# Cross-attention with low-rank updates: value and denominator products of a half batch as one run, and key parts placed by transfers on chip

## The reference

```python
def lin(x, W, A, B):          # low-rank update, R = 16
    return x @ W + 2.0 * (x @ A @ B)
q = lin(x, Wq, Aq, Bq)        # 32 heads
k = lin(ctx, Wk, Ak, Bk)      # 8 heads, each serves 4 query heads
v = lin(ctx, Wv, Av, Bv)
p = softmax(q @ k.T / sqrt(32))
out = x + lin(concat_heads(p @ v), Wo, Ao, Bo)
```

## Time and profile before

| | us |
|---|---|
| median of 3 runs | 1055.89 |
| runs | 1052.37 to 1056.95 |
| the profiled execution | 1049.1 |
| its span, first to last instruction | 1047.3 |
| TensorE busy | 989.5 (94% of the span) |
| VectorE busy | 581.6 (56%) |
| ScalarE busy | 497.8 (48%) |
| GpSimd busy | 286.3 (27%) |
| mean granted TensorE clock | 0.982 |

### The profile page before, as it was taken

How to read it: one execution, slowest core, us unless ns; L and a number is a source line. 1 busy time by engine, 2 the same in 40 slices (tenths; PEclk the granted TensorE clock), 3 DMA queues, 4 the chain that set the end, 5 groups by cost and what they waited for, 6 DMA issues and landing times.

```text
span 1047.3 us, 15736 instructions
## 1 busy us (share of the span) xinstructions
PE 989.5 (94%) x5904; PEld 781.7 (75%) x5904; DVE 581.6 (56%) x1005; ACT 497.8 (48%) x971; POOL 286.3 (27%) x84
## 2 busy tenths in 40 slices
PE   6989999999999999999999999999999877999998
PEld 4879999977777777777777777777777534678886
DVE  5661322378666666666667666667667645233321
ACT  3341221336666666666667667667667434201000
POOL 1201000001434434533533543443443345300000
PEclk9999999999999999999999999999999968999999
DMA  6739522363423423333323324325223251567652
GB/s 184 229 97 248 157 89 97 107 146 91 117 51 96 103 66 95 97 74 96 96 68 101 97 53 116 86 48 132 78 55 74 71 147 40 164 212 211 201 160 80
DMA packets 104467, 118.56 MB, mean 113 GB/s; under 512 B 29536, under 2 KB 89056, under 8 KB 104400
## 3 DMA queue, kind: packets, MB, share of 16 engines
q1 hardware_dynamic: 100540, 104.00, 37.4%
q10 hardware_dynamic: 3860, 13.67, 3.6%
HBM read 87.59 MB, written 29.82 MB: 112 GB/s over the span
## 4 chain that ended last, share of the span: by engine, by line
PE 77%; DVE 7%; ACT 7%; issue 6%; DMA 3%; SPq 0%; ACTq 0%; POOL 0%; DVEq 0%; POOLq 0%
PE ps L664 12%; PE ps L666 12%; PE ps L665 12%; PE ps L854 8%; PE ps L869 8%; PE ps L843 7%; PE ps L749 4%; PE ps L804 3%; PE ps L808 3%; PE ps L806 3%; ACT k_stack L978 2%; ACT probs L1038 2%; PE ps L905 2%; DVE ct_lo L1169 1%; DMA out_dram<-residual 1%
## 5 line engine op out<-in xcount | busy, mean ns | idle before, releaser
L1247 DVE TENSOR_REDUCE maxima<-ps 112x1 f32<-112x375 f32 x512 | 270.7, 542 | 105.5 <-PE ps L854 99.0
L1038 ACT ACTIVATE probs<-ps 125x448 f32<-125x448 f32 x384 | 207.0, 544 | 129.3 <-PE ps L843 124.9
L645 POOL TENSOR_TENSOR prob_sum<-probs 125x1792 f32<-125x1792 f32 x32 | 129.3, 4039 | 377.8 <-ACT probs L1038 377.8
L854 PE MATMUL ps<-k_stack,q_stack 96*112 96x376 f32 x512 | 187.9, 367 | 7.6 <-DVE maxima L1247 5.8
L843 PE MATMUL ps<-q_stack,k_stack 97*125 97x448 f32 x384 | 147.3, 384 | 11.4 <-ACT probs L1038 11.1
L854 PEld LDWEIGHTS ps<-k_stack,q_stack 96*112 96x112 f32 x512 | 90.5, 177 | 84.7 <-DVE maxima L1247 69.2
L650 POOL TENSOR_TENSOR prob_sum<-prob_sum,probs 125x1792 f32<-125x1792 f32 x32 | 128.9, 4029 | 34.5 <-ACT probs L1038 34.5
L978 ACT ACTIVATE k_stack<-ps 32x376 fp32r<-32x376 f32 x256 | 121.6, 475 | 9.9 <-PE ps L666 6.1
L804 PE MATMUL ps<-wv_hi,ct_hi 128*125 128x256 f32 x384 | 111.7, 291 | 0.5 <-DVE k_stack L1174 0.5
L808 PE MATMUL ps<-wv_hi,ct_lo 128*125 128x256 f32 x384 | 107.8, 281 | 0.0
L806 PE MATMUL ps<-wv_lo,ct_hi 128*125 128x256 f32 x384 | 107.7, 281 | 0.0
(11 more groups left out here) (80 smaller groups left out, 1457.9 us busy)
## 6 DMA issues: line engine op xcount, KB each, us to landing
ctx_in<-in_ctx_dram SPq DMA_DIRECT2D x16, 1344.0 KB
q_stack<-q_scratch SPq DMA_DIRECT2D x96, 224.0 KB, 3.7
x_in<-in_x_dram SPq DMA_DIRECT2D x8, 896.0 KB, 8.6
q_scratch<-q_out_hi SPq DMA_DIRECT2D x16, 448.0 KB, 2.8
q_scratch<-q_out_lo SPq DMA_DIRECT2D x16, 448.0 KB, 3.8
attn_scratch<-attn SPq DMA_DIRECT2D x32, 224.0 KB, 4.0
attn_rows<-attn_scratch SPq DMA_DIRECT2D x14, 512.0 KB, 4.7
inv_tile<-inv_scratch SPq DMA_DIRECT2D x56, 128.0 KB, 4.8
```

Source lines behind the costliest of these rows:

```text
L854: mm = pe.matmul(ps[0:NQ, NAT + i % 2, 0:NTE], qst[nxt][0:STK, g, rr * NQ:(rr + 1) * NQ], kst[nxt][0:STK, g, :], start=True, stop=True)
L1038: act.activation(probs[:, c, j, :], ps[0:TR, score_bank(i), 0:QH], ACT.Exp, scale=SM).then_inc(exp_done, 1)
L1247: dve.tensor_reduce(maxima[:, h, i:i + 1], ps[0:NQ, NAT + i % 2, 0:NT], AX.X, ALU.max).then_inc(max_done, 1)
```

## The change

P becomes one piece at 0.815 of the half: it waits for all twelve exponentials, does the twelve value products and then, in the same run, the half's own denominators. GpSimd's sums are done per head (eight operations of 448 columns). Denominators are copied and stored at the start of the next half (A and D at 0.005). The rest of the plan is drawn in: S every 0.065 instead of 0.07, N every 0.045 instead of 0.052, M at 0.805. S1 uses bank DEN too. Keys: ScalarE copies the hi part of four heads at once to a buffer, VectorE writes the remainder of four heads to another, and SP issues 12 transfers per half (three parts, four heads, 32 rows of 1504 bytes) from there to `k_stack`. E0/F0 stand at 0.55, never ahead of K0.7, E1/F1 at the end of the second half (before: spread over the next first half). The context load is issued after the transfers of half 0. The buffers lie where the query outputs were, so ScalarE's wait for their stores moves ahead of the steps.

```diff
 STK = 3 * HD
 NS = TC * JH
+SUMS = 2 * JH
...
+K_PLACED = 16 * 3 * JH
...
-S_IN_DEN = (3, 5, 7, 9, 11)
+S_IN_DEN = (1, 3, 5, 7, 9, 11)
...
-    [("S", i, 0.01 + 0.07 * i) for i in range(TC * JH)]
-    + [("P", 0, 0.31), ("P", 1, 0.583), ("P", 2, 0.925), ("A", 0, 0.048), ("D", 0, 0.097)]
+    [("S", i, 0.01 + 0.065 * i) for i in range(TC * JH)]
+    + [("A", 0, 0.005), ("D", 0, 0.005), ("P", 0, 0.815)]
     + [("I", 0, 0.35), ("J", 0, 0.45)]
-    + [("N", i, 0.03 + 0.052 * i) for i in range(JH * RH)] + [("M", 0, 0.925)]
-    + [("E0", j, 0.62 + 0.08 * j) for j in range(JH)] + [("E1", j, 0.03 + 0.06 * j) for j in range(JH)]
-    + [("F0", j, 0.62 + 0.08 * j) for j in range(JH)] + [("F1", j, 0.03 + 0.06 * j) for j in range(JH)],
+    + [("N", i, 0.02 + 0.045 * i) for i in range(JH * RH)] + [("M", 0, 0.805)]
+    + [("E0", 0, 0.55), ("F0", 0, 0.55), ("E1", 0, 0.82), ("F1", 0, 0.82)],
     key=lambda item: item[2])
...
         order.append(piece)
         at += COST[piece[0]]
+        if piece[0] == "K" and piece[2] == KC - 1:
+            early = [item for item in order if item[0] in (f"E{piece[1]}", f"F{piece[1]}")]
+            order = [item for item in order if item not in early] + early
...
+            def place_k(b, half):
+                at_least(sp, st_done, NS * (2 * (b - 2) + half + 1))
+                for part in range(3):
+                    if part == 2:
+                        sp.wait_ge(k_lo_set, 2 * b + half + 1)
+                    else:
+                        sp.wait_ge(k_hi_set, 2 * b + half + 1)
+                    t = (kev_lo if part == 2 else kev_hi)[half]
+                    for j in range(JH):
+                        sp.dma_start(kst[b % 2][HD * part:HD * (part + 1), half * JH + j, :].bitcast(F32),
+                                     t[HD * j:HD * (j + 1), :].bitcast(F32)).then_inc(k_in[half][b % 2], 16)
...
                         elif kind == "D":
+                            if "G" in has[h]:
+                                at_least(sp, den_stored, 16 * 2 * b)
                             store_den(sp, 2 * b + h - 1, b - 1 + h, 1 - h)
...
-                        elif kind == "K" and i == 1 and k == 0 and "C" in has[h]:
-                            sp.wait_ge(ct_turned, (b + 3) * KC)
-                            load_ctx(b + 3)
+                        elif kind == "F0":
+                            place_k(b + 2, 0)
+                            if "C" in has[h]:
+                                sp.wait_ge(ct_turned, (b + 3) * KC)
+                                load_ctx(b + 3)
+                        elif kind == "F1":
+                            place_k(b + 2, 1)
...
-                        if kind == "S" and i == 2 * JH - 1:
-                            at_least(pool, den_done, n)
-                            pool.wait_ge(exp_done, NS * n + 2 * JH)
-                            pool.tensor_tensor(prob_sum[:, :, :], probs[:, 0, :, :], probs[:, 1, :, :], ALU.add
+                        if kind == "S" and JH <= i < 2 * JH:
+                            j = i - JH
+                            if j == 0:
+                                at_least(pool, den_done, n)
+                            pool.wait_ge(exp_done, NS * n + i + 1)
+                            pool.tensor_tensor(prob_sum[:, j, :], probs[:, 0, j, :], probs[:, 1, j, :], ALU.add
                                                ).then_inc(psum_added, 1)
...
                             if i == 0:
                                 pe.wait_ge(q_in[h][nxt], 48 * (pair + (off + 1) // 2 + 1))
-                                pe.wait_ge(k_lo_set, JH * (m + 1))
+                                pe.wait_ge(k_in[h][nxt], K_PLACED * (pair + (off + 1) // 2 + 1))
...
                         elif kind == "P":
-                            pe.wait_ge(exp_done, NS * n + JH * (i + 1))
...
-                        elif kind == "D":
-                            denominators(n - 1)
+                            pe.wait_ge(exp_done, NS * (n + 1))
+                            at_least(pe, attn_set, n)
+                            pe.wait_ge(v_set, 2 * (b + 1))
+                            for c in range(TC):
+                                for j in range(JH):
+                                    g = h * JH + j
+                                    mm = pe.matmul(ps[HD * j:HD * (j + 1), CTX, 0:QH],
+                                                   v_sb[cur][:, c, g * HD:(g + 1) * HD], probs[:, c, j, :],
+                                                   start=(c == 0), stop=(c == TC - 1))
+                                mm.then_inc(pv_done, 1)
+                            denominators(n)
...
-            def k_hi(b, par, half, j):
+            def k_hi(b, half):
                 act.wait_ge(k_done, 2 * b + half + 1)
-                at_least(act, st_done, NS * (2 * (b - 2) + half + 1))
-                for quad in range(2):
-                    op = act.activation(kst[par][HD * quad:HD * (quad + 1), half * JH + j, :],
-                                        ps[HD * j:HD * (j + 1), (VA, TURN)[half], 0:NTE], ACT.Copy)
-                op.then_inc(k_hi_set, 1)
+                if b:
+                    act.wait_ge(k_in[half][(b - 1) % 2], K_PLACED * ((b + 1) // 2))
+                act.activation(kev_hi[half][:, :], ps[:, (VA, TURN)[half], 0:NTE], ACT.Copy).then_inc(k_hi_set, 1)
...
+            def k_lo(b, half):
+                at_least(dve, st_done, NS * (2 * (b - 2) + half + 1))
+                dve.wait_ge(k_hi_set, 2 * b + half + 1)
+                dve.tensor_tensor(kev_lo[half][:, :], ps[:, (VA, TURN)[half], 0:NTE], kev_hi[half][:, :],
+                                  ALU.subtract).then_inc(k_lo_set, 1)
```

More of the change, by code:

```diff
@@ L113, in half_order @@
         at += COST[piece[0]]
+        if piece[0] == "K" and piece[2] == KC - 1:
+            early = [item for item in order if item[0] in (f"E{piece[1]}", f"F{piece[1]}")]
+            order = [item for item in order if item not in early] + early
     order += [(kind, i, 0) for kind, i, _ in plan]
-    assert "K" not in has or order.index(("K", 0, KC - 1)) < order.index(("E0", 0, 0))
+    for half in range(HALVES if "K" in has else 0):
+        assert order.index(("K", half, KC - 1)) < order.index((f"E{half}", 0, 0))
     return order + [("E", 0, 0)]
@@ L222, in xattn_kernel @@
         raw2, wsum2, ast2, bst2, at = staging("_o", r_x)
+        kev_hi, kev_lo = [None, None], [None, None]
+        for half in range(HALVES):
+            kev_hi[half], at = place(f"k_out_hi{half}", [P, NTE], F32R, at)
+            kev_lo[half], at = place(f"k_out_lo{half}", [P, NTE], F32R, at)
         assert at <= top[0]
@@ L289, in xattn_kernel @@
         k_lo_set = sem("k_lo_set")
+        k_in = [[sem(f"k_in{h}{par}") for par in range(2)] for h in range(HALVES)]
         v_done = sem("v_done")
@@ L383, in run_steps @@
         def run_steps(eng, step, wo_factors):
-            full = ({"A", "D", "V", "T", "N", "Q", "E1"}, {"A", "D", "G", "T", "K", "C", "N", "Q"})
+            full = ({"A", "D", "V", "T", "N", "Q"}, {"A", "D", "G", "T", "K", "C", "N", "Q"})
             step(-1, 0, (set(), {"K"}))
-            step(-1, 1, ({"V", "T", "N", "E1"}, {"T", "K", "C", "N"}))
+            step(-1, 1, ({"V", "T", "N"}, {"T", "K", "C", "N"}))
             wo_factors()
@@ L861, in step @@
                         elif kind == "P":
-                            pe.wait_ge(exp_done, NS * n + JH * (i + 1))
-                            if i == 0:
-                                at_least(pe, attn_set, n)
-                                pe.wait_ge(v_set, 2 * (b + 1))
-                            for j in range(JH):
-                                g = h * JH + j
-                                mm = pe.matmul(ps[HD * j:HD * (j + 1), CTX, 0:QH],
-                                               v_sb[cur][:, i, g * HD:(g + 1) * HD], probs[:, i, j, :],
-                                               start=(i == 0), stop=(i == TC - 1))
-                            mm.then_inc(pv_done, 1)
-                        elif kind == "D":
-                            denominators(n - 1)
+                            pe.wait_ge(exp_done, NS * (n + 1))
[9 more added lines that the diff above has]
+                            denominators(n)
                         elif kind == "W":
@@ L912, in _ @@
             run_steps(pe, step, wo_factors)
-            denominators(2 * B - 1)
             def tile(pair, par):
@@ L1072, in wo_factors @@
             def wo_factors():
-                for par in range(2):
-                    act.wait_ge(q_stored[par], GROUPS * QS // 2 * 32)
                 ab_hi(W_O, CTX)
+            for par in range(2):
+                act.wait_ge(q_stored[par], GROUPS * QS // 2 * 32)
             run_steps(act, step, wo_factors)
```

40 lines of the change are left out of this document (16 added, 24 removed).

## The result

The changed kernel takes 1082.5 us (median; 1081.0 to 1085.3) against 1055.9 before: 1.028 of it, 95% interval 1.025 to 1.031. The forecast was 1046.5, its range ended at 1066, and 0.56 stood on faster. It is slower. The span of the profiled execution is 1083.5 us against 1047.3, the mean granted clock 0.966 against 0.982.

The account below looks back on a forecast made before the run. TensorE was taken to set the pace through the steady steps. 1049.1 - 27.0 - 0.9 + 18.5 = 1039.7 us for the profiled execution, 1046.5 on the median; range 1028 to 1066.

Parts of the forecast that it names:

- The steady halves: Batches in steady work: 40.09 - 1.80 - 1.43 + 1.30 = 38.16 us each; 14 save 27.0, batch 14's first half 0.9.
- the 1.5 of batch 0: First half of batch 0: copy, twelve issues and landing take 7.6 us against 6.1 of work, costing 1.5 us.
- The transfers on chip: SP's twelve key transfers a half, 0.46 us an issue: N0 loses 0.1 us a batch, context covered with 0.8 left.
- rival (c): SP's issuing sets the pace: at 0.57 an issue the keys' twelfth transfer is 1.2 us late for N0; 1063.5 us, chance 0.16.
- The landing: Key transfers land 1.9 us from issue; the context load is done 6.2 us after its issue ended, before T0 needs it.
- The merged run: Value and denominator products as one run of eight passes, 3.42 us instead of 4.32 a half; saves 1.80 a batch.
- New idle on the maxima: Denser packing makes N wait for max reductions behind VectorE's remainders: 0.9 at N5, 0.3 at N14 a batch.
- the waits above: Waits the move takes away: T5 0.43, N5 0.30 and the P0 behind it 0.70, together 1.43 us a batch.
- The start: First N0 waits 16.2 us for key placements queued behind query and context loads; with clock and other terms 18.5 us.
- Rival (a): At the start, the placements don't stand behind the query loads: 17.7 us less, 1029 us, chance 0.10.
- Issuing is cheap: The skill's rule on DMA initiation; forecast disagreed, 5.5 us of issuing against two of bytes; by the rule 1.4 us lower.
- The last three halves: Halves at the end, bound by other engines' chain: no change priced, within 5 us either way.

Follow-up runs that it names:

- the best kernel: Changed kernel with early placement of half 0's keys, start's placement ahead of loads, second hi part issued by GpSimd, old order in output-weights half: 1017.0 us, 0.966.
- The experiment on their order: Against the changed kernel with earlier placement, second half's later and start reordered: S and N of the output-weights half drawn to 0.55 of their times; 1040.2 us, 0.987.

## Why the prediction was wrong

The span was forecast at 1047.3 - 9.4 = 1037.9 and is 1083.5: 45.6 too little; on the medians it is 1082.5 - 1046.5 = 36.0. By its own steps, on the marks above:

- **The steady halves: 37.9 of the 45.6.** Forecast for the 14 batches, the half behind them and the 1.5 of batch 0: -26.4; measured +1.2 + 12.1 - 1.8 = +11.5. The step that failed is "The transfers on chip": SP's queue ahead of N0 and T0 was seen there, priced at 0.1 a batch, and costs 1.72 + 1.48 = 3.2. Two sizes in it are wrong. The issue: "Nearest is the 32-row one", 0.46, a transfer from memory; it is 0.62. In the half shown, twelve end 8.9 us after S8 and not some 7, and land at 10.4 instead of 8.4; N0's slot, 8.96 after S8, was right (8.65 forecast). So N0, which "clears it by a hair", waits 1.4, and in the four halves where the twelve took 8.1 to 8.8 us it waits 2.2 to 2.8. That is rival (c), whose mechanism and place were right and whose price stopped at 0.57; at 0.62 its own formula gives 11 x 0.16 = 1.8 a batch, so 14 x 1.8 = 25, for 14 x 1.72 = 24 measured. That alone would have given 1046.5 + 25 = 1071. The landing: the context was to be there 6.2 us after its issue ended, read from where its bytes stop in a stretch in which nobody waited for it. Its user starts 8.2 after the end of the issue, with the placements behind it or without. In the half shown its issue ended 10.0 us after S8, 2.1 later than forecast, and it was usable at 19.2 instead of 14.1. T0's slot moved as well, from 14.9 to 16.7 (1.4 of it N0's wait): "Covered, with 0.8 us left" became 2.5 of wait here and 1.48 on average. That second wait I had as no rival at all: I priced the issuing for its first user and gave the second only the better end. In all, 13 first halves took 3.9 more than by the terms, 50 us, and 13 second halves 1.0 less (the point on the maxima), 13 us. First halves without either wait take 19.04 in the best kernel, 0.5 above the terms without the 0.1; where that lies stays open.
- **The merged run: right.** 3.14 us from its first start to the next ordinary one, for 7 x 0.39 + 0.50 = 3.23 by the earlier trace rows. The second halves, without a queue at their door, gained 1.14.
- **New idle on the maxima: wrong for the kernel as built.** 1.2 of the 1.3 a batch was put in second halves, which were to take 19.64 - 0.90 - 0.43 + 1.2 = 19.5; they take 18.50, and no wait on the maxima shows in them. The relief that was "priced at nothing beyond the waits above" is what paid it: the merge without the transfers shows those waits (19.17 and 20.73), with them it does not. I had treated the two parts of the change as additive, and they are not: of the second halves' 1.14 the merge alone gains 0.47 and the transfers alone 0.02.
- **The start: right in cause and nearly in size.** Forecast 17.0 up to and with the half of step -1, measured 19.0 + 0.6. N0 was to stand at 227.2 and stood at 229.7; of its terms, no row showed the "0.5 to land", and the last placement landed 9.5 us after its issue, 3 to 4 after the engines had been full. The Trainium skill (DMA: Bandwidth & Descriptors, Queues, rings and completion order) has each engine consume its descriptors in ring order. The runs agree for transfers within SBUF: the placement landed at 229.7 behind the loads and at 219.7, 10 us earlier, when it was issued ahead of them. Rival (a) is out.
- **Issuing is cheap: not here.** The Trainium skill (DMA: Bandwidth & Descriptors, Issuing engines are not separate DMA queues) calls the time to initiate a DMA usually small relative to the DMA itself, and the prediction set a row against that. Twelve issues take 7.5 us for 0.56 MB, and taking four of them off SP removed N0's wait and shortened T0's with the bytes unchanged. The same passage says that issuing on several engines saves only the issuing sequencer's time. The runs agree: what was gained was SP's time, and the context took no less time to land (9.0 against 8.2 us).
- **The last three halves, "nothing, within 5": 5.2 lost in the profiled execution** (+4.2 in the half with the output weights, +1.0 behind it). The experiment on their order says that the 4.2 is a mark that moved. From the start of that half to the end it is 223.6 us before and 228.8 after, but in the eleven experiments it is anything from 223.6 to 228.8, and 223.6 in the kernel with the second half's placement later, whose order there is that of the changed kernel. So the 5.2 is within the spread of single executions of this part, and no loss by the change is shown in it. It is part of the 10 us by which the spans differ more than the medians.

The terms sum: 37.9 + 2.6 (start) + 5.2 = 45.7.

## What to carry to other kernels

Price a queue for every user behind it. An issue that moves ahead of a load delays that load's user too, so write down, for each item of the queue, its slot, its landing and its user's slot, in a changed plan that may have moved the users earlier. A clearance smaller than what the spread of the issue price makes over the whole row (here 11 x (0.62 - 0.46) = 1.8 us against 0.25) is a wait in the forecast.

A part's total can hide what it is worth: the transfers alone came to 1.010, with a start of some 20 us lost and a gain of 0.9 in each first half that a wait took back. The merge alone came to 0.995, and both with the queue mended to 0.966. (The transfers alone with the mended queue were not run, so how much of the 3.4% needs both parts isn't shown.) Before judging such a change, move the transfer to the first point at which its data is ready: two numbers in the plan were worth 28 us. And read a wait over all its repetitions: the half shown above had a T0 wait of 2.5 us where the mean is 1.5.

## What the runs showed that was not expected

- For the same 32-row transfer within SBUF an issue took 0.62 us on SP, 0.67 on average (0.61 to 0.84) on ScalarE and 0.50 on GpSimd. On SP it rises at times. Two rows of its queue in the changed kernel:

```profile
515.80 3.56 SPq L542 DMA_DIRECT2D k_stack<-k_out_lo  x4
...
549.44 3.53 SPq L542 DMA_DIRECT2D k_stack<-k_out_lo  x4
```

Both are 0.88 or 0.89 each. The DMA share was 0.92 in the first stretch and 0.22 in the second, so full transfer engines don't explain it; what does isn't shown.
- GpSimd's sum of a quarter (448 columns) takes 1.155 us, above a quarter of the 4.04 of the whole; its busy time went from 286 to 319 us.
- A wait in full work can be paid a second time: in two of the 13 first halves TensorE came back from T0's wait at the lower of its levels, with a pitch of 0.21 instead of 0.12 us, some 1.3 us more each. Eleven others, with one wait up to 2.8 us, kept the upper one.
